# Attention of a three-layer kernel on one core: maxima and scores contract over 64 rows, in opposite halves of the array

## The reference

```
q = x @ Wq.T                                   # 4 groups x 8 heads x 16 features
k = x @ Wk.T ; v = x @ Wv.T                    # 8 heads x 16 features
scores = einsum('bsqhd,bthd->bqhst', qh, kh) * scale
probs  = softmax(scores, axis=-1)
a_dot  = einsum('bqhst,bthd->bsqhd', probs, vh)
...
out = a_dot * (1 - w) + a_mem * w
```

## Times and profile before

| | us |
|---|---|
| median of 3 executions | 5355.58 |
| lowest and highest | 5353.96 and 5367.55 |
| the profiled execution | 5345.12 |
| its span, first to last instruction | 5343.3 |
| PE busy in the span | 4804.8 |
| DVE busy | 3613.9 |
| ACT busy | 2391.2 |

### The profile page before, as it was taken

How to read it: one execution, slowest core, us unless ns; L and a number is a source line. 1 busy time by engine, 2 the same in 40 slices (tenths; PEclk the granted TensorE clock), 3 DMA queues, 4 the chain that set the end, 5 groups by cost and what they waited for, 6 DMA issues and landing times.

```text
span 5343.3 us, 143989 instructions
## 1 busy us (share of the span) xinstructions
PE 4804.8 (90%) x62912; PEld 3484.9 (65%) x62912; DVE 3613.9 (68%) x7890; ACT 2391.2 (45%) x4592; POOL 712.5 (13%) x909
## 2 busy tenths in 40 slices
PE   4799999999999984899999999999989989989988
PEld 4678777777777773565665665565566566566564
DVE  3677766667776772766766766766767766766765
ACT  2333334333343332545545545545545545545545
POOL 0000000000000001121121121121121121021021
PEclk9899999999999996999999999999999999999999
DMA  1232222222222222000000000000000000000000
GB/s 59 55 74 59 59 67 67 71 59 59 63 70 71 59 63 69 1 17 1 17 17 2 17 17 1 17 17 1 17 17 1 17 17 2 17 17 1 17 9 9
DMA packets 352131, 171.72 MB, mean 32 GB/s; under 512 B 300016, under 2 KB 300784, under 8 KB 350736
## 3 DMA queue, kind: packets, MB, share of 16 engines
q1 hardware_dynamic: 342528, 145.20, 10.2%
q10 hardware_dynamic: 8976, 17.30, 1.1%
HBM read 93.74 MB, written 67.63 MB: 30 GB/s over the span
## 4 chain that ended last, share of the span: by engine, by line
PE 45%; DVE 10%; ACT 3%; issue 1%; DMA 1%; POOL 0%; SPq 0%; DVEq 0%; ACTq 0%; POOLq 0%
PE row_psum L1625 9%; PE row_psum L1614 8%; PE row_psum L1601 8%; DVE smax L1884 5%; PE row_psum L40 5%; PE row_psum L42 5%; PE row_psum L41 5%; PE row_psum L1656 1%; PE row_psum L1674 1%; ACT probs L1361 1%; DVE xr_lo L1750 1%; DVE probs L1864 1%; PE row_psum L1568 1%; PE row_psum L1424 1%; PE row_psum L1569 1%
## 5 line engine op out<-in xcount | busy, mean ns | idle before, releaser
L1884 DVE TENSOR_REDUCE smax<-row_psum 128x1 f32<-128x512 f32 x2048 | 1260.8, 683 | 300.2 <-PE row_psum L1601 299.6
L1361 ACT ACTIVATE probs<-row_psum 128x512 f32<-128x512 f32 x2048 | 1076.2, 607 | 589.1 <-PE row_psum L1614 367.9
L1601 PE MATMUL row_psum<-k_stack,q_stack 128*128 128x512 f32 x2048 | 864.0, 433 | 24.5 <-DVE smax L1884 24.4
L1614 PE MATMUL row_psum<-q_stack,k_stack 128*128 128x512 f32 x2048 | 843.9, 424 | 25.2 <-ACT probs L1361 19.3
L1601 PEld LDWEIGHTS row_psum<-k_stack,q_stack 128*128 128x128 f32 x2048 | 392.9, 193 | 343.9 <-DVE smax L1884 244.9
L1614 PEld LDWEIGHTS row_psum<-q_stack,k_stack 128*128 128x128 f32 x2048 | 381.7, 189 | 269.8 <-ACT probs L1361 163.6
L1625 PE MATMUL row_psum<-probs,v_aug 128*32 128x512 f32 x4096 | 489.2, 598 | 0.0
L868 DVE TENSOR_TENSOR lane_t<-lane_t,lane_p 128x30 f32<-128x30 f32 (+14 forms) x960 | 318.5, 332 | 32.9
L865 DVE TENSOR_TENSOR lane_p<-lane_t 128x30 f32<-128x30 f32 (+14 forms) x960 | 316.2, 329 | 23.5
L40 PE MATMUL span_bank<-x_hi,w_hi 128*128 128x256 f32 x1024 | 301.5, 294 | 30.9 <-DVE x_lo L841 30.9
L40 PE MATMUL row_psum<-wf_hi,xr_hi 128*128 128x320 f32 (+1 forms) x1024 | 324.8, 317 | 0.5 <-DVE xr_lo L1750 0.3
(11 more groups left out here) (209 smaller groups left out, 9765.0 us busy)
## 6 DMA issues: line engine op xcount, KB each, us to landing
x_sp<-in_x ACTq DMA_DIRECT2D x33, 512.0 KB, 3.9
tri_dram<-tri SPq DMA_DIRECT2D x256, 64.0 KB, 2.0
lane_t<-tri_dram SPq DMA_DIRECT2D x32, 512.0 KB, 4.6
inv_dram<-lane_t SPq DMA_DIRECT2D x32, 512.0 KB, 2.6
inv_b<-inv_dram SPq DMA_DIRECT2D x256, 64.0 KB, 2.3
x_res<-in_x SPq DMA_DIRECT2D x32, 512.0 KB, 3.8
x<-x_res SPq DMA_DIRECT2D x32, 512.0 KB, 3.8
xs<-x SPq DMA_DIRECT2D x16, 1024.0 KB, 5.5
```

The source lines that it names most:

```text
L1361: act.activation(probs[:, h % PROBS, tt, :], ps[:, m % STACK_BANKS, :], ACT.Exp, scale=float(DH) ** -0.5).then_inc(exp_ready, 1)
L1601: pe.matmul(ps[:, STACK_BANKS + m % MAX_BANKS, :], q_stack[:, qt, P * st:P * st + P], k_stack[:, kv, :], start=True, stop=True).then_inc(m ...
L1614: pe.matmul(ps[:, m % STACK_BANKS, :], k_stack[:, kv, P * tt:P * tt + P], q_stack[:, qt, :], start=True, stop=True).then_inc(score_mm, 1)
L1884: dve.tensor_reduce(smax[:, g, st:st + 1], ps[:, STACK_BANKS + (NT * g + st) % MAX_BANKS, :], AX.X, ALU.max).then_inc(max_ready, 1)
```

## The change

A helper `rows_of` gives the 64 rows of a key head, or all 128. `maximum` uses the 64 rows from step 7 on, `score` for the heads below 25: these are the steps 7 to 31, in which a maximum and a score stand next to each other. The maxima of steps 0 to 6 and the scores of steps 32 to 38 keep 128 rows. Results are the same, since the rows left out were multiplied by zeros.

```diff
+            def rows_of(kv, paired):
+
+                return slice(64 * (kv % 2), 64 * (kv % 2) + 64) if paired else slice(0, P)
+
             def attention(b, following):
...
-                    pe.matmul(ps[:, STACK_BANKS + m % MAX_BANKS, :], q_stack[:, qt, P * st:P * st + P], k_stack[:, kv, :],
+                    rows = rows_of(kv, g >= SCORE_LAG)
+                    pe.matmul(ps[:, STACK_BANKS + m % MAX_BANKS, :], q_stack[rows, qt, P * st:P * st + P], k_stack[rows, kv, :],
                               start=True, stop=True).then_inc(max_mm, 1)
...
-                    pe.matmul(ps[:, m % STACK_BANKS, :], k_stack[:, kv, P * tt:P * tt + P], q_stack[:, qt, :],
+                    rows = rows_of(kv, h + SCORE_LAG < NH)
+                    pe.matmul(ps[:, m % STACK_BANKS, :], k_stack[rows, kv, P * tt:P * tt + P], q_stack[rows, qt, :],
                               start=True, stop=True).then_inc(score_mm, 1)
```

## The result

The changed kernel takes 5389.28 us (median of 15 runs, 5376.7 to 5398.99), the kernel before in the same runs 5367.55 (15 runs, 5346.77 to 5378.6). The ratio is 1.0041, 95% interval [1.0027, 1.0054]: 22 us slower. The profiled execution of after took 5376.7 us, span 5374.9.

A forecast was written before the change was run, and what follows sets the result against it. ACT and DVE, not PE alone, were taken to bound the rounds, DVE the stretch ahead. From 5345.1 us, gains of 18.4 and 4.7 and a clock loss of 16.2 gave 5338.2, as a median 5349; range 5320 to 5378.

The forecast's parts named there:

- the slower cases: Rivals: clock falls in the rounds too, 5383 us, chance 0.14; pairs hardly overlap or tile changes cost more, 5357 to 5360, 0.08.
- The signs that I named: Pair starts within 0.05 us; A 3.05; B 5.58; av_n wait every round; clock 0.50; first values block over 1.85.
- the price of the slow clock in the stretch: Ahead of the first round: 1.2 GHz costs nothing there and saves 0.93 us in five batches, 4.7 us.
- What bounds the kernel: In the rounds ACT, then PE's order, sets A and DVE sets B; DVE alone paces the stretch ahead of them.
- A: From first values block's end to the second's start, five per batch: 3.28 us becomes 3.05, 18.4 us gained in all.
- B: From second values block's end to the maxima's transposes: DVE's length, stays 5.58 us, no gain, 0.01 at most.
- what comes late next: At the end of B, av_n: PE would wait for it some 0.2 us per round.
- Changes of tile: Around the turn and ahead of the maxima's transposes: 0.1 us each, hidden by av_n's wait; uncovered 24 us in all.
- the rival that I gave 0.08: Pairs hardly overlap or tile changes cost another 0.1 us each: A loses 0.07 per round; 5357 to 5360 us, chance 0.08.
- The DVE-paced stretch: Ahead of the first round, 16 reduces take 9.66 us without a gap: no gain from faster pairs.
- The clock at the third transposes and V0: At the stretch's end, slow transposes and first values block lose 1.35 us in 12 of 16 batches, 16.2 us.
- The rounds: Rival: in A and B the clock falls behind half-height pairs too, 34 us on top, 5383 us; chance 0.14.

The follow-up runs named there:

- e5: Against the kernel before: 64 rows only for the six pairs from the first to the second block of values in each round; ratio 0.9997.
- e4: The changed kernel with only the maxima on 64 rows, the scores kept at 128; ratio to the kernel before 1.1473.
- e2: The changed kernel with 64 rows only in steps 7 to 12, 128 from step 13 on; ratio to the kernel before 1.0058.
- e9: Kernel before plus 64-row pairs between the values blocks only, seven extra matmuls ahead of second transposes and ten at each attention's start; ratio 0.9929.
- e11: The changed kernel plus seven extra matmuls ahead of the second transposes and ten in the wait at each attention's start; ratio to the kernel before 0.9995.
- e1: The changed kernel with 64 rows only from step 13 on, 128 in steps 7 to 12; ratio to the kernel before 1.0008.
- e10: Against the kernel before: 64 rows from step 14 on, except in the pairs between the first and second values blocks of each round; ratio 1.0095.
- e12: The kernel before plus seven extra matmuls ahead of the second transposes and ten at each attention's start, no 64-row tile; ratio 0.9958.
- e7: The kernel before plus seven extra 128-row matmuls in the 2.0 us wait ahead of the second transposes; ratio 1.0009.
- e3: The changed kernel plus two extra 64-row matmuls behind each pair in steps 9 to 12; ratio to the kernel before 1.0076.

## Why the prediction was wrong

I forecast no change, 5349 us, and the kernel is slower by 0.41%. The median of 5389 us lies past the range's end of 5378. Of that, 12 us are the kernel before itself, whose median over more runs is 5367.55 and not the 5355.58 that I had worked from; by the ratio alone, 1.0041 x 5355.58 = 5377.5, the time is at the very end of the range, on the side of the slower cases. The signs that I named all came, and the sum was still wrong. The step that failed is the price of the slow clock in the stretch, which I put at less than nothing (4.7 us saved; the stretches came out 9.6 us dearer); beside it, the untouched rest of the layer, which I put at nothing, took 15 us more. Point by point:

- *What bounds the kernel, and A.* Right. 3.07 us for 3.05, with ACT's first exp at 0.57 for 0.56. A full-clock round takes 12.88 instead of 13.09; over five rounds and 16 batches that is 17 us (65.46 less 64.40, times 16) where the sum had 18.4. e5 shows it in all 80 rounds.
- *B and what comes late next.* Right: 5.58 us, and PE waits 0.21 us for av_n in 60 of 64 later rounds.
- *Changes of tile.* Costed at 0.1 us and hidden: nothing of them is seen in after. But where every matmul changes its tile, e4 has 0.20 us each, twice my figure. On the path, at that size, the rival that I gave 0.08 would have been dearer than I wrote. The Trainium skill, "TensorEngine Tiling (Array Packing)", Tiling Modes, has the drain at a change of mode; this case's size of it is now 0.20 us.
- *The DVE-paced stretch.* "No gain" held, but "in the stretch that costs nothing, and it saves the 0.93 us of the five batches" did not. DVE's 16 reduces do take 9.66 us as before; in the batch shown they start 0.92 us later. This is the step that failed. I had reckoned with slow transposes at the third ones only. The second ones of the earlier trace rows at 2210.60 already took 1.01 in before, and in 12 of after's batches they are slow as well (0.93 to 1.01 us), and DVE waits for the first maximum behind them: such a stretch takes 10.3 to 10.4 us, the other four 9.7. The mean is 10.24 against 9.64, 9.6 us in all where I had 4.7 less: 14.3 us of the error.
- *The clock at the third transposes and V0.* The fall itself was forecast, and e2, e9 and e11 show that the pairs bring it. I took 12 batches at 1.35 us, 16.2 us; against a full-clock round of 12.88 the first round loses 1.26 us in the mean of all 16 batches (slow in 15), 20.2 us. That is within my 4 to 32 and 4.0 us of the error. The size came out near for a reason that was wrong: "a slow spell of 3.3 us", from the earlier trace rows at 2412, is not what the changed work shows. The clock stays down from the second transposes to V0 in the window above, so the spell reaches V0 in 15 of 16 batches. But it ends before V0 does, and V0 loses 0.71 us in the mean where I had 0.85. That the two meet is luck. The row at 1239, where 32-row tiles at 5.00 of 5.00 us busy were followed by the slow clock, was a hint; I used it for whether the clock falls and not for how long. Stretch and first round together, measured against a full clock (9.36 and 12.88 us), lose 34 us.
- *The rounds.* In after only 4 of 64 later rounds are over 13.2 us, 3 us in all (51.70 less 51.52, times 16). As a price this rival was far too high, 34 us. Its mechanism is real, though, and depends on what stands before: 13 of 64 in e1, 36 of 64 in e10.
- *What the sum left out.* The rest of the layer, with no tile of the change in it, took 0.95 us more per batch, 15 us, nearly as large as my whole clock term. It is the same clock behind another wait, in before too; I had read only the five slow stretches of before and not its 16 slow starts (31.2 or 32.2) and its rests. Whether the change causes it is not settled. By the table the rest ranges from 92.6 to 94.0 in kernels that don't touch it, 92.98 and 93.16 in e12 and e7 without any 64-row tile; so at least part of the 15 us is where the batches came to lie.

The account, for the profiled executions: -17.0 (A) -4.5 (the slow stretches of before, which are inside the 34) +34.2 (the clock in stretch and first round) +2.9 (later rounds) -1.4 (starts) +15.2 (rest) = 29 us, where my sum had -6.9. With my terms alone, but the clock's at its measured size (-17.0 -4.5 +34.2), it would be 13 us slower, just under the 16 that a measurement here can tell.

The Trainium skill, "TensorE: Matmul & The Clock Gate", section "HAM oscillation — how this bites in real kernels", puts a clock that falls in mid-kernel down to waits in which TensorE idles between its bursts. That agrees with the two waits that e9 fills: with them filled the clock holds in all its starts and stretches. It doesn't cover e11, where the clock falls with both waits filled and no wait over 0.33 us in the 6.1 us ahead of the fall. Here the measurement decides: behind half-height pairs the clock can fall without a long wait.

## What to carry to other kernels

Packing two half-height matmuls pays only where PE's start of the work is what the next engine waits for (here six pairs of sixteen in a round), and everywhere else it only leaves the array with less to do; put it at those places alone, with full-height work (V here) close on both sides. When the clock is a term of the sum, ask how long it stays down with the changed work, and read all its waits and not only the ones beside the edit. A wait of 2 to 3 us on PE that recurs in each stage can be filled with matmuls nobody reads: two fillings gave 0.4% here and made the starts and stretches of all batches alike, and with the packing at the right place 0.7%. One filling alone (e7) gave nothing in the total, since the clock fell more often elsewhere.

## What the hardware showed that I had not expected

- The two matmuls of a pair on 64 rows each start within 0.01 us of each other and the next pair 0.23 us later (3655.38 to 3655.61 in after): twice the rate in full. Alternating 64 and 128 rows costs 0.43 us per matmul instead of 0.23, and 0.72 at 1.2 GHz.
- The granted clock fell behind 64-row pairs with no wait of PE over 0.33 us in the 6.1 us before (e11). In after it stayed at 1.2 GHz from the second transposes until within the first V0, over 13 us with no gap in PE's rows; in e4, with 64 and 128 rows in turn, it stayed there for 23.7 us. With two more 64-row matmuls behind each pair (e3) it rose earlier, within the stretch.
- After the same wait of 1.99 us, with the same 128-row work behind it, the clock fell in some batches and not in others, and in e2 strictly in every second one. What sets that, beyond the moment, stays open.
